# Attention step of a gated cross-attention and feed-forward kernel, reordered over its step boundary

## The reference

```python
def xattn(q, k, v):                      # (32, 64, 512) each; k = v = context; HEADS = 8, DH = 64
    qh, kh, vh = (einsum('bcn,oc->bon', t, W).reshape(b, 8, 64, 512) for t, W in ((q, Wq), (k, Wk), (v, Wv)))
    qh = softmax(qh, axis=-2) * 64 ** -0.5          # over the 64 features of a head
    kh = softmax(kh, axis=-1)                       # over the 512 positions
    context = einsum('bhdn,bhen->bhde', kh, vh)
    out = einsum('bhde,bhdn->bhen', context, qh).reshape(b, 512, 512)
    out = einsum('bcn,oc->bon', out, Wo) + bo
    return out / max(sqrt(sum(out * out, axis=1)), 1e-12) * g * 8
x = x + tanh(g_xattn) * xattn(layernorm(x), ctx, ctx)
x = x + tanh(g_ffn) * ffn(layernorm(x))             # ffn: 4-bit weights, 512 -> 1376 (silu(gate) * up) -> 512
```

## Time and profile before

| | |
|---|---|
| median of three runs | 686.7 us |
| span of the profiled execution | 684.8 us (its granted TensorE clock 0.992 on average) |
| TensorE / weight loads | 664.9 us (97%) / 350.7 us (51%) |
| VectorE | 594.3 us (87%) |
| ScalarE | 468.0 us (68%) |
| POOL | 360.1 us (53%) |
| the chain that ended last | PE 86%, ACT 5%, DVE 5%, issue 1%, DMA 1%, POOL 1% |
| `fold_context` L1150, 180 to 204 us | 32 records in one step, 1.08 us to the next group |
| steady step | 24.36 us |

### The profile page before, as it was taken

The page is one execution under the profiler, slowest core; times in us unless marked ns, Lnnn a source line. Parts: engine busy times, 40 slices in busy tenths (PEclk is TensorE's granted clock), DMA queues, the critical chain, the costliest instruction groups (busy, mean ns, idle before and its releaser), DMA issues.

```text
span 684.8 us, 14670 instructions
## 1 busy us (share of the span) xinstructions
PE 664.9 (97%) x5141; PEld 350.7 (51%) x5141; DVE 594.3 (87%) x815; ACT 468.0 (68%) x822; POOL 360.1 (53%) x434
## 2 busy tenths in 40 slices
PE   7899999999999999999999998999999999999995
PEld 6454565466455546545645533445444544454443
DVE  7777898899889889888987858999999999989987
ACT  4887677678677767767866756677665766666663
POOL 6213323223232422323236476698878877887885
PEclk8999999999999999999999999999999999999998
DMA  4122331330332122023110100000000001000102
GB/s 116 37 55 50 99 80 22 101 95 22 82 95 57 46 82 78 7 83 79 35 52 23 27 7 2 1 1 1 1 32 32 1 1 46 17 2 15 47 1 62
DMA packets 32046, 28.97 MB, mean 42 GB/s; under 512 B 20047, under 2 KB 22234, under 8 KB 32002
## 3 DMA queue, kind: packets, MB, share of 16 engines
q1 hardware_dynamic: 29594, 27.73, 14.8%
q10 hardware_dynamic: 2408, 0.70, 0.4%
HBM read 22.42 MB, written 4.23 MB: 39 GB/s over the span
## 4 chain that ended last, share of the span: by engine, by line
PE 86%; ACT 5%; DVE 5%; issue 1%; DMA 1%; POOL 1%; ACTq 0%; SPq 0%; DVEq 0%; POOLq 0%
PE pair L1395 8%; PE pair L1184 8%; PE small L1112 8%; PE small L1078 7%; PE pair L1396 7%; PE pair L1064 6%; ACT eq L713 4%; PE small L1096 4%; PE pair L1419 4%; PE pair L1431 4%; PE small L1395 4%; PE small L1396 4%; PE pair L1209 3%; PE pair L1043 3%; PE small L1150 3%; PE pair L1194 2%
## 5 line engine op out<-in xcount | busy, mean ns | idle before, releaser
L1800 DVE SCALAR_TENSOR_TENSOR acc<-pair,scale_T,acc 128x512 f32<-128x512 f32 (+1 forms) x176 | 131.7, 748 | 15.3 <-ACT acc L855 2.0
L614 POOL TENSOR_TENSOR yT<-yT,y_scaled 128x512 f32<-128x512 f32 (+1 forms) x78 | 100.4, 1288 | 4.6 <-ACT y_scaled L880 3.8
L704 ACT ACTIVATE ek<-pair,kneg 128x512 f32<-128x512 f32 x128 | 86.3, 682 | 18.0 <-DVE kneg L1661 18.0
L1395 PE MATMUL pair<-ek,w_gu 128*128 128x512 f16 (+1 forms) x235 | 91.3, 388 | 1.8 <-DVE acc L1800 1.4
L1396 PE MATMUL pair<-ekT,w_gu 128*128 128x512 f16 (+1 forms) x235 | 89.0, 379 | 0.0
L1666 DVE TENSOR_TENSOR eq<-eq,pair 128x1024 f32<-128x1024 f32 x64 | 77.8, 1216 | 11.2 <-PE pair L1169 11.0
L1656 DVE TENSOR_REDUCE qmax<-pair 128x16 f32<-128x1024 f32 x64 | 78.2, 1222 | 8.5 <-PE pair L1043 7.6
L1661 DVE TENSOR_REDUCE kneg<-pair 128x2 f32<-128x1024 f32 x64 | 77.9, 1218 | 0.9 <-PE pair L1064 0.6
L1419 PE MATMUL pair<-in_hi,d_int 128*128 128x512 f32 (+1 forms) x132 | 75.8, 575 | 1.3 <-DVE yT L1839 1.3
L592 POOL TENSOR_TENSOR inter<-act_gate,acc 128x512 f32<-128x512 f32 (+1 forms) x43 | 55.1, 1281 | 40.5 <-DVE acc L1800 16.7
L713 ACT ACTIVATE eq<-pair 128x1024 f32<-128x1024 f32 x64 | 65.8, 1028 | 15.2 <-PE pair L1194 15.1
(11 more groups left out here) (205 smaller groups left out, 1463.9 us busy)
## 6 DMA issues: line engine op xcount, KB each, us to landing
xall<-in_x SPq DMA_DIRECT2D x16, 256.0 KB, 2.8
ctx_raw<-in_ctx SPq DMA_DIRECT2D x16, 256.0 KB, 3.0
out_x<-xall SPq DMA_DIRECT2D x16, 256.0 KB, 2.0
zero<-zeros_plus SPq DMA_DIRECT2D x8, 344.0 KB, 5.3
packed<-in_L_ffn_gate_qweight SPq DMA_DIRECT2D x4, 688.0 KB
packed<-in_L_ffn_up_qweight SPq DMA_DIRECT2D x4, 688.0 KB
packed<-in_L_ffn_down_qweight SPq DMA_DIRECT2D x10, 256.0 KB
zero<-zeros_plus SPq DMA_DIRECT2D x5, 256.0 KB, 4.9
```

Source lines behind the costliest of these rows:

```text
L614: pool.tensor_tensor(yT16[:, nt, :] if it == IT - 1 else total, total, y_scaled[:, nt, :], ALU.add).then_inc(z_add, 1)
L704: act.activation(ek[:, b, t, :], k_pairs[t % 2][:, b, :], ACT.Exp, bias=kneg[:, b, t:t + 1], scale=-1.0, accum_out=ksum[:, k_slot(b, t):k_ ...
L1395: pe.matmul(gu_bank[count % 3][0:w, :], lhsT, xT_hi[:, g, rows], start=True, stop=False)
L1800: dve.scalar_tensor_tensor(out=acc[0:w, n % 2, m, :], in0=gu_bank[(8 * n + job) % 3][0:w, :], scalar=scale_T[0:w, it, 4 * m + g:4 * m + g ...
```

## The change

The order of the attention step changes over its boundary, on all engines:

- TensorE: a step begins with `t_logits(0)`, `denominators()`, `k_transposed(3, back=1)` of the pair before, `spread_inverse_norm()` (for pair p - 3, one step later than before, into `small[1]`) and only then `k_logits(0)`. Before, `k_transposed(3)` and `spread_inverse_norm` closed the step before, and `k_logits(0)` stood ahead of `denominators`. The step ends with `k_transposed(2)`.
- Banks: `q_logits(3)` is made in `act_pair`, `k_transposed(2)` in `k_pair`. So `q_logits(3)` waits for the move out of `k_transposed(1)`, and no longer for `q_exp_tile(2)`.
- `k_transposed(0)` stands ahead of `fold_context()`; the wait for `kctxT` stands ahead of its last slot.
- `fold_context()` multiplies quads: 64 rows by 64 columns, without the zero rows, batch 0 into `small[0]`, batch 1 into `small[1]`. The number of matmuls stays 16. Both banks are now one tensor, `small_pair`.
- `ctx_transposed()` and `context_rows()` are one piece for both batches (8 transposes, one copy of 128x512), after `less_max(2)`; the copy stands between `normalise(2)` and the second `less_zero`.
- VectorE: `normed_output` and `gated` (two operations) become `normed_and_gated` (one, third in the step); the sum with the residual goes to POOL (`residual_added`, 128x512). `second_stats` moves behind `reciprocals`. In the drain `reciprocals` comes before `second_stats`.
- ScalarE: `k_exps(3)` ahead of `context()`; `q_exp_tile(3)` ahead of the move out of `k_transposed(2)`; that of `k_transposed(3)` behind the one of the denominators of the next step, in the drain too, there ahead of its two DMAs.
- POOL: in the drain `residual_added(13)` stands ahead of `ffn_normalised(2)`.

```diff
-        small = [st.enter_context(nc.psum_tensor(f"small{i}", [P, 512], F32)) for i in range(2)]
+        small_pair = st.enter_context(nc.psum_tensor("small_pair", [P, 2, 512], F32))
+        small = [small_pair[:, i, :] for i in range(2)]
...
+        q_pairs = [k_pair, k_pair, k_pair, act_pair]
+        kT_pairs = [act_pair, act_pair, k_pair, act_pair]
...
+            def residual_added(k):
+                pool.wait_ge(yn_ready, k + 1)
+                pool.tensor_tensor(xall[:, k, :], xall[:, k, :], yn[:, :], ALU.add).then_inc(x1_done, 1)
...
+                    if residual and at_least(p, 3):
+                        residual_added(p - 3)
...
             step(PAIRS - 1, 1, True, False)
-            pool.wait_ge(ct_mm, 2 * PAIRS)
+            residual_added(PAIRS - 3)
+            pool.wait_ge(ct_mm, PAIRS)
             ffn_normalised(2)
...
-                    act.activation(ekT[:, t, :, :], act_pair[:, :, :], ACT.Copy).then_inc(kt_evac, 1)
+                    act.activation(ekT[:, t, :, :], kT_pairs[t][:, :, :], ACT.Copy).then_inc(kt_evac, 1)
...
-                    act.activation(eq[:, par, t, :, :], k_pair[:, :, :], ACT.Exp).then_inc(q_exp, 1)
+                    act.activation(eq[:, par, t, :, :], q_pairs[t][:, :, :], ACT.Exp).then_inc(q_exp, 1)
...
                 if drain and combine:
                     denominators()
+                    k_transposed(3, back=1)
                     act.wait_ge(d_evac, PAIRS)
...
                 denominators()
-                if not residual:
-                    k_transposed(3, back=1)
+                k_transposed(3, back=1)
                 k_exps(0)
                 if not residual:
                     gates()
...
                 if residual:
                     squared_norms()
                     q_maxima()
+                    k_exps(3)
                     context()
                 else:
                     context()
                     q_maxima()
-                k_exps(3)
-                for t in range(NT):
-                    q_exp_tile(t)
-                    k_transposed(t)
+                    k_exps(3)
+                q_exp_tile(0)
+                k_transposed(0)
+                q_exp_tile(1)
+                k_transposed(1)
+                q_exp_tile(2)
+                q_exp_tile(3)
+                k_transposed(2)
...
-                            pe.wait_ge(q_exp, 4 * p)
+                            pe.wait_ge(kt_evac, 4 * p - 1)
...
+                    if not drain:
+                        for t in range(OT):
+                            for b in range(2):
+                                for e in range(2):
+                                    last = pe.matmul(small[b][half(e), t * C:(t + 1) * C],
+                                                     kctxT[half(b), t * P + e * DH:t * P + (e + 1) * DH],
+                                                     foldT[half(b), b, 2 * t + e, :], start=True, stop=True)
+                        last.then_inc(m_mm, 1)
+                        return
...
-                            if b and t == OT - 1 and project:
-                                pe.wait_ge(k_exp, 8 * p + 8)
...
+                    elif t == 3:
+                        pe.wait_ge(kt_evac, 4 * p + 2)
...
                 def k_transposed(t, back=0):
+                    if not project and not back:
+                        return
+                    pe.wait_ge(pool_consts, 2)
+                    if t >= 2:
+                        pe.wait_ge(q_exp, 4 * (p - back) + t + 1)
+                    elif t:
+                        pe.wait_ge(kt_evac, 4 * p + 1)
+                    else:
+                        pe.wait_ge(k_done, p + 1)
+                    for slot in range(2 * OT):
+                        b, ot = divmod(slot, OT)
+                        if combine and t == 0 and slot == 2 * OT - 1:
+                            pe.wait_ge(pool_consts, 2)
+                            pe.wait_ge(a_evac, r + 1)
+                            if residual:
+                                pe.wait_ge(ss_evac, r)
+                        for e in range(2):
+                            last = pe.transpose(kT_pairs[t][:, e, slot * DH:(slot + 1) * DH],
+                                                ek[half(e), b, ot, t * P:(t + 1) * P], ident[half(e), half(e)])
+                    last.then_inc(kt_mm, 1)
+
+                def ctx_transposed():
+
                     if not project:
                         return
                     pe.wait_ge(pool_consts, 2)
-                    if t > 0:
-                        pe.wait_ge(kt_evac, 4 * (p - back) + t)
-                    elif not combine:
-                        pe.wait_ge(k_exp, 8 * p + 8)
-                    for slot in range(2 * OT):
-                        b, ot = divmod(slot, OT)
-                        for e in range(2):
-                            last = pe.transpose(act_pair[:, e, slot * DH:(slot + 1) * DH],
-                                                ek[half(e), b, ot, t * P:(t + 1) * P], ident[half(e), half(e)])
-                    last.then_inc(kt_mm, 1)
-
-                def ctx_transposed(b):
-
-                    if not project:
+                    if combine:
+                        pe.wait_ge(m_evac, r + 1)
+                    else:
+                        pe.wait_ge(fold_ready, 4)
+                    for t in range(NT):
+                        for b in range(2):
+                            last = pe.transpose(small[b][:, t * C:(t + 1) * C], ctx_raw[half(b), par, t * P:(t + 1) * P],
+                                                ident[half(b), half(b)])
+                    last.then_inc(ct_mm, 1)
+
+                def spread_inverse_norm():
+                    if not at_least(p, 3):
                         return
-                    pe.wait_ge(pool_consts, 2)
-                    if not combine:
-                        pe.wait_ge(fold_ready, 4)
-                    elif b:
-                        pe.wait_ge(m_evac, r + 1)
-                    elif residual:
-                        pe.wait_ge(ss_evac, r)
-                    else:
-                        pe.wait_ge(ct_evac, 2 * r + 2)
-                    for t in range(NT):
-                        last = pe.transpose(small[1 - b][:, t * C:(t + 1) * C], ctx_raw[half(b), par, t * P:(t + 1) * P],
-                                            ident[half(b), half(b)])
-                    last.then_inc(ct_mm, 1)
-
-                def spread_inverse_norm():
-                    if not residual:
-                        return
-                    if isinstance(p, int) and p == 2:
+                    if isinstance(p, int) and p == 3:
                         pe.wait_ge(wT_ready, 3)
-                    pe.wait_ge(rn_gathered, 32 * r)
-                    pe.wait_ge(ct_evac, 2 * p + 1)
-                    pe.matmul(small[0][:, :], spread_batch[0:C, :], rn_rows[0:C, :], start=True, stop=True).then_inc(rn_mm, 1)
+                    pe.wait_ge(rn_gathered, 32 * (p - 2))
+                    pe.wait_ge(ct_evac, r + 1)
+                    pe.matmul(small[1][:, :], spread_batch[0:C, :], rn_rows[0:C, :], start=True, stop=True).then_inc(rn_mm, 1)
...
                 t_logits(0)
+                denominators()
+                k_transposed(3, back=1)
+                spread_inverse_norm()
                 k_logits(0)
-                denominators()
                 t_logits(1)
                 k_logits(1)
                 output(0)
...
                 q_logits(0)
                 spread_reciprocals(0)
                 less_max(0)
+                k_transposed(0)
                 fold_context()
-                k_transposed(0)
                 spread_reciprocals(1)
                 q_logits(1)
                 less_max(1)
                 k_transposed(1)
                 spread_reciprocals(2)
-                ctx_transposed(1)
                 q_logits(2)
                 less_max(2)
-                k_transposed(2)
-                ctx_transposed(0)
+                ctx_transposed()
                 spread_reciprocals(3)
                 q_logits(3)
                 less_max(3)
-                spread_inverse_norm()
-                k_transposed(3)
+                k_transposed(2)
...
                 if project:
                     q_maxima(0)
-                    k_maxima(0)
                     if not last:
                         layernorm_stats(p + 1, i + par, 1 - par)
+                    if at_least(p, 3):
+                        normed_and_gated(p - 3)
+                    k_maxima(0)
                     q_maxima(1)
                     k_maxima(1)
                     if not last:
                         layernorm_apply(p + 1)
                     reciprocals()
+                    if at_least(p, 3):
+                        second_stats(p - 3)
                     q_maxima(2)
                     k_maxima(2)
                     q_maxima(3)
-                    if at_least(p, 3):
```

(11 more changed lines are left out.)

103 lines of the change are left out of this document (49 added, 54 removed).

## The result

The changed kernel takes 696.8 us (median, 696.1 to 697.6) where the kernel before takes 686.9 beside it: a ratio of 1.014 (95% interval 1.013 to 1.016), 10 us slower. The profiled execution has a span of 695.8 us against 684.8.

What follows compares the result with a forecast made beforehand. It took TensorE's work as the bound before, VectorE reaching the boundary together with it. Loop +0.5, last step -0.7, step 2 -0.2 and drain +2.8 gave +2.4 on 686.7: 689.1 us, range 683.5 to 694.5.

Steps and rivals of the forecast that it cites:

- The boundary: From the end of less_max(0) to t_logits(0): 8.05 us after the change against 8.16 before, TensorE waiting for normalise(3).
- The fold: fold_context in quads on TensorE: 0.85 us taken for 1.08 before, with 0.54 and 1.08 as ends.
- the branch through the exponential: Boundary chain through ScalarE's exponential, q_logits(2), ctx_transposed, VectorE's copy, less_zero and normalise(3): 7.2 us plus the fold.
- the one through VectorE's queue: Boundary chain all on VectorE from the fold to normalise(3): 6.99 us plus the fold, 0.2 less than the other.
- VectorE takes TensorE's place as the bound: The forecast case: VectorE bounds the step boundary and POOL is late in the drain, 689.1 us, chance 0.42.
- Rival 2: At the boundary normalise 0 to 3 run without waits, VectorE's work alone counts: 681.4 us, chance 0.18.
- rival 3: The fold stays at 1.08 us and the drain costs its full 4.4: 693.6 us, chance 0.20.
- From `t_logits(0)` to X: Rest of the step, up to the end of less_max(0): 16.40 us after the change against 16.20 before.
- No cost: VectorE from t_logits(0) to less_max(0): later k_logits(0) and denominators 1.1 us earlier were said to cost nothing.
- The last step: End of the last step: q_exp_tile(3) follows the other exponential by 1.60 us, before 2.32; -0.7 us for the drain's denominators.
- The drain: Hand-over to the feed-forward part: POOL waits ahead of ffn_normalised(2), costing between 1.4 and 4.4 us, middle +2.8.
- Rival 4: The drain swallows POOL's delay and only the level loop's change is left: 686.3 us, chance 0.20.

Runs made afterwards that it cites:

- less_zero_early: The changed kernel with VectorE's first less_zero moved ahead of normalise(0): 696.2 us, 1.0135 of the kernel before.
- less_zero_pair: The changed kernel with the first less_zero moved ahead of normalise(0) and the second to behind normalise(1): 689.4 us, 1.0033 of the kernel before.
- after_old_fold: The changed kernel with the fold as before, 128 rows with the zero rows, all into small[0]: 702.0 us, 1.0219 of the kernel before.
- xlow_waits: The changed kernel with POOL's x_low waiting until VectorE has done the reciprocals: 691.7 us, 1.0068 of the kernel before.
- The two experiments on the kernel before: The kernel before with both less_zero moved forward, 693.6 us, and with the second alone moved forward, 688.7 us.
- pool_late_sum: The changed kernel, in the drain POOL's residual_added(13) behind ffn_normalised(3) and second_stats ahead of reciprocals: 693.3 us, 1.0093 of the kernel before.

## Why the prediction was wrong

It said 689.1, 683.5 to 694.5, and slower as the likeliest sign. The time lies 7.7 above the forecast and 2.3 above the range. The sign was right, but only in part for the reasons given: of the 10 us the forecast had 2.4, and 4.5 to 5 come from an effect that it didn't have.

**The boundary** was right. From X, the end of `less_max(0)`, to `t_logits(0)` it forecast 8.05; measured 201.21 - 193.28 = 7.93. The fold, for which it took 0.85 between 0.54 and 1.08, came at 0.66, and the chain with it as forecast (7.2 + 0.66 = 7.86). The forecast's limit was there too: the group behind the fold waits for `normalise(0)`, from 0.66 down and not from 0.75. The fold's own 0.63 is nearer to the end of 0.54 than to the middle that was taken, and below the 0.80 that was given as an estimate. The idle time of TensorE there, some 1.1 forecast, is 0.87 to 0.96, released by the operation that was named; the 0.2 between steps of 688 and 512 columns is there. That the branch through the exponential sets the time, and the one through VectorE's queue ends a little earlier, is what less_zero_early and less_zero_pair showed, though the text's heading for it ("VectorE takes TensorE's place as the bound") said too much: it is one operation in a chain of three engines. Rival 2 (waits vanish) failed for the reason given against it, rival 3 (quads do nothing) by the 0.66 and by after_old_fold, where the old fold costs 0.42 a step.

**From `t_logits(0)` to X** it forecast 16.40; measured 193.28 - 176.66 = 16.62. Two small things: `k_logits(1)` seems to wait for the move of `k_transposed(3)` out of its bank, which ScalarE ends at 205.27, 0.05 ahead of the start at 205.32, some 0.1 in all; and the -0.08 for the change of shape behind `less_max(0)` isn't seen. A level step is 24.6 and not 24.45. xlow_waits, which has only such steps, takes 342.5 for the 14 where the kernel before takes 341.0: +1.5, against +0.5 less 0.2 forecast. That is 1.2 of the 7.7, of which the 0.1 is read and the rest is not taken apart.

**The step that failed** is the "No cost" in the part from `t_logits(0)` to X, said of the denominators that come 1.1 us earlier and of `reciprocals`, which waits for their DMAs. Their wait was counted as slack, and what it kept apart was not asked. In its place VectorE's `rden_parts` met POOL's `x_low` in six steps and took 1.05 to 1.30 instead of 0.20 to 0.23: 4.5 us by the traces, 5 by the medians. The last sentence of the prediction named the right kind of failure but looked beside POOL's new sum, and not beside an old operation that now falls together with another one. It adds that no row shows a changed length. None of the rows chosen does, but the trace that they were taken from has POOL's 0.87 for 0.20 in the steady step and the CAST's 0.61 for 0.20 in step 1.

**Steps 0 and 1** were not costed. From the first kinv to the second it takes 26.7 to 27.4 us in the changed kernel and the experiments on it that leave step 1 alone, and 25.7 in the kernel before, 1.0 to 1.7 more. But the 25.7 is one execution. The two experiments on the kernel before, which have its steps 0 and 1, took 26.2 and 27.4; in them the granted clock was at the lower level from 15 to nearly 22 and to nearly 26 us, in the kernel before only up to 15. So the price of the change here is not shown well. One part is read: `q_logits(3)` of step 0 waits 1.2 us for ScalarE's move out of `k_transposed(1)`, through the bank that the change gave it; before, 0.3 for the exponential. A second is the wait of `k_maxima(0)` behind the transposes. How they add up stays open.

**The last step** was right: 1.47 between the two last query exponentials against 1.60 forecast and 2.32 before.

**The drain** has the right sum, +2.9 from the last exponential on against +2.8, and that is partly luck. POOL's delay was right: `inverse_norm(14)` came 4.5 later, 4.4 forecast. But TensorE was to stand for up to 4.4 ahead of its spread, and 2.8 was the middle of two ends. It stands for 1.03 there, because it comes 2.2 later itself, and 1.43 of that is the wait for the last multiplication behind the long `bound_norms`: the effect that the forecast didn't have, once more. The two DMAs behind ScalarE's extra move issued while it ran (0 of 0 to 0.9). Rival 4 (the drain swallows the delay) is out by pool_late_sum.

The range was too narrow because none of its cases had this cost. In the steady step before, the same effect cost nothing that could be seen (TensorE did not wait for the spread that POOL's long operation leads to).

## What to carry to other kernels

When a change makes a producer earlier, look up every wait that it shortens, and list what the other engines do in the time into which the waiting work moves: a VectorE operation between SBUF tensors and a GpSimd operation on SBUF should be put in order by a semaphore where they may meet on the chain that sets the time. Look in the trace before for one operation that has two lengths: there an effect shows itself while it is still free. Before calling an engine the bound, follow the chain that ends at the wait: here moving either of two equal `less_zero` alone gained next to nothing, and moving both gained 0.78 us a step. A change that loses by itself can be worth keeping: what it frees (1.12 us ahead of `normalise(0)`) has to be spent by a second edit.

## What the runs showed of the hardware that I had not expected

- A VectorE TENSOR_TENSOR of 0.23 us between SBUF tensors took 1.30, and a CAST of 0.20 took 1.05, beside a POOL operation that had started first; the RECIPROCAL (0.55) and `normalise`, which reads PSUM for one of its inputs (1.22), did not change. In the drain a TENSOR_SCALAR on 8 columns took 1.89 for 0.16 beside POOL's `plain_scaled`. The other way round, a POOL TENSOR_TENSOR on 8 columns took 0.74 to 0.94 for 0.20 beside `less_zero`. None of this shows as idle time: the held operation only looks long and ends with the other.
- Matmuls of 64 rows by 64 columns in four quads start their 32 records within 0.48 us, on average 0.015 apart, four every 0.058; with all 128 rows, as before, the 32 take 0.93, on average 0.030 apart, two every 0.058. About 0.15 more passes in both before the group of the next shape starts, which is why 1.08 became 0.63 and not half of it. The Trainium skill, "TensorE: Matmul & The Clock Gate", section "Wait — 56ns, not 53.3ns?", gives about 25 ns as the least distance of two starts; for records that go to different quads this trace shows less, and the measurement decides.
